# Scaled row maxima, reordered rotations and early loads in the 8-head layers of a four-part network

## The chip, the cores and the metric

The kernel runs on one core of a Trainium2 chip. The metric is the device time of one execution in microseconds. TensorE multiplies matrices, VectorE (DVE), ScalarE (ACT) and GpSimd (POOL) do the elementwise work, and SyncE (SP) issues transfers. Each engine works through its own list in order and waits on semaphores.

## The reference, cut to what matters

```python
x = x + attention0(layernorm(x))          # (8, 512, 256), one head, decay
x = x + experts(layernorm(x))             # 8 experts, one chosen for each row
x = x + attention1(layernorm(x))          # 16 heads of 16, causal
h = layernorm(x)
for l in range(2):                        # the 8-head layers: 8 heads of 64
    q, k, v = split(shift_token(h) @ wqkv[l])
    q, k = l2norm(q) * qs[l], l2norm(k) * ks[l]       # per head
    q, k = rotary_xpos(q, k)
    sim = 8 * q @ k.T                     # own window of 128 and the one before, causal
    h = h + softmax(sim) @ v @ wo[l]
    u = layernorm(shift_token(h)) * ln_g[l] + ln_b[l]
    a, g = split(u @ w1[l] + b1[l])       # 2 x 682
    h = h + (a * gelu(g)) @ w2[l] + b2[l]
x = x + h
```

## The kernel before, in words

Four phases follow one another, each a function with a block of instructions for every engine, and a barrier of all engines between them: `phase_attn0`, the routing and the experts, `phase_attn1` (the 16-head attention) and `phase_layers` (the two 8-head layers). The change touches the last two.

`phase_attn1` takes the 8 sequences in four trips of two. Its SP block (L877 to L892) loads the next trip's rows, then for each of 8 groups of heads copies rows of maxima into the queries' tile (L886), and stores its two results `x3_d` and `y_d[0]`. The second is what the layers start from. Its projection weights `w`, its rows `came` and `rows_of` (even and odd trips use different tiles) are allocated at the head of the phase.

`phase_layers` runs 16 sequences one after another (8 for each layer; `n` counts them, `HALVES` is 16). Nothing is planned by a program: the order on each engine is written out by hand in a loop over `n`. In its turn `n` an engine does the attention of sequence `n`, the feed-forward part of sequence `n - 1` and the projection of sequence `n + 1`, mixed in a fixed order. Products are made of three TensorE passes on high and low parts of both operands (`product`, L2116 to L2118).

The projection of a sequence has four tiles of 128 rows. For each tile TensorE makes queries, keys and values (`project`), ScalarE squares queries and keys (L1955) and takes the square root of the summed squares (`square_root`, L1967), VectorE turns queries and keys by rope (`turn`, L1712 and L1714), sums the squares (`norms`, L1722 and L1723) and inverts the lengths (`invert`, L1728), GpSimd adds the two halves of the turn (`add`, L1591) and scales the keys by their inverse lengths (`scale_keys`, L1529), and TensorE transposes both (`flip_qk`, L2165). The queries are not scaled: their inverse length goes into the softmax. `rotations` on each engine holds this order for tiles 1 to 3; `between` in it is the place where the normalised rows of the feed-forward part are handled (`high_rows` on ScalarE, L2045 and L2049, `low_rows` on VectorE, L1836).

The attention has 8 steps, each one window of four heads. In step `j` TensorE makes scores (L2191), VectorE adds the mask and takes four row maxima (L1771, a custom instruction that reads the scores in PSUM), then multiplies them by minus the query's inverse length (`scaled_bias`, L1766, two instructions of two columns), ScalarE takes four exponentials with that as bias and the inverse length as scale (L2001), VectorE inverts the four sums (L1779), GpSimd scales the probabilities (L1619), TensorE transposes them (L2212), ScalarE and VectorE copy them out (L2013, L1750), TensorE multiplies by the values (L2231), and after every second step ScalarE copies the result (`oT_out`, L2019). Between these TensorE has the 12 hidden products of the feed-forward part of sequence `n - 1` (L2116 to L2118). Gelu (L2033), the high and low parts of its result (L2038, L1799), the product with `wo` (L2244), the residual (L1805), the shift by one row (L2251, L2252) and the contraction with `w2` follow. GpSimd also splits `w1` and `w2` in high and low parts, once for each layer (L1640, L1643).

The phase starts with transfers of the first two sequences' rows, of `wqkv`, rope and two scale rows, then of the other weights. ScalarE waits for rope, scales and `wqkv` together (`FIRST_ALL`) before it makes the first high part (L2054).

## Time and profile before

| | |
|---|---|
| three runs | 2630.89, 2639.43, 2642.0 us; median 2639.43 |
| the profiled execution | 2633.45 us, its span 2631.7 us |
| TensorE busy | 2300.4 us, 87% of the span |
| VectorE, ScalarE, GpSimd busy | 1592.2 (60%), 1357.9 (52%), 920.2 us (35%) |
| mean granted TensorE clock | 0.932 |
| the 8-head layers | from 1208 us to the end, 54% of the span |
| one sequence in them | about 84 to 85 us |

The span is the time from the first to the last instruction in the trace; the execution is a little longer. Busy shares are averages over phases with different limits, so the rows below come from the layers themselves. An engine's line in a timeline gives, in brackets, how long it sat idle before that instruction and what ended the wait.

### The profile page before, as it was taken

How to read it: one execution, taken by the hardware profiler on the slowest of the kernel's cores; microseconds unless marked ns; L12 is line 12 of the kernel's file. 1: busy time of each engine (PE TensorE's matmuls, PEld its weight loads, DVE VectorE, ACT ScalarE, POOL GpSimd, SP SyncE). 2: the span in 40 equal slices, each digit the busy share in tenths (PEclk: the TensorE clock that was granted, in tenths of full speed). 3: DMA queues.
4: the chain of work that ended last, by engine and by line, in shares of the span. 5: the costliest groups of instructions: out<-in, count | busy, mean ns of one | idle time of the engine just before them, and what ended most of it. 6: DMA issues, size and time to landing. Idle time of an engine off the chain costs nothing.

```text
span 2631.7 us, 45273 instructions
## 1 busy us (share of the span) xinstructions
PE 2300.4 (87%) x15746; PEld 1744.6 (66%) x15746; DVE 1592.2 (60%) x5017; ACT 1357.9 (52%) x3211; POOL 920.2 (35%) x1363
## 2 busy tenths in 40 slices
PE   7999599996887878885789999999998899999997
PEld 4666599984454544534567777777767777777776
DVE  5565422225757666656567766677767766677664
ACT  1111233334656465562575567655775567566663
POOL 2221222205334343332444334433454434434441
PEclk9999799997887878787799999999999999999998
DMA  3222311102010100003000000000101000000000
GB/s 127 96 97 92 123 37 37 37 27 85 4 49 18 50 18 10 25 3 125 9 1 17 17 17 1 17 17 17 50 33 37 25 18 9 25 25 25 1 17 24
DMA packets 75937, 96.40 MB, mean 37 GB/s; under 512 B 6113, under 2 KB 69090, under 8 KB 75458
## 3 DMA queue, kind: packets, MB, share of 16 engines
q1 hardware_dynamic: 70786, 81.89, 9.2%
q0 software_dynamic: 3408, 9.31, 1.2%
q8 instruction: 130, 2.13, 0.3%
q10 hardware_dynamic: 1520, 2.31, 0.2%
q14 instruction: 93, 0.76, 0.1%
HBM read 62.69 MB, written 30.28 MB: 35 GB/s over the span
## 4 chain that ended last, share of the span: by engine, by line
PE 34%; ACT 8%; DVE 7%; issue 2%; POOL 2%; DMA 0%; SPq 0%; DVEq 0%; ACTq 0%
PE l_free L2116 5%; PE l_free L2117 5%; PE l_free L2118 5%; PE l_score L2244 4%; PE l_out L2231 3%; ACT l_probs L2001 3%; PE l_score L2191 3%; PE l_turned L2212 2%; PE l_turned L2116 2%; PE l_turned L2118 2%; PE l_turned L2117 2%; DVE l_probs L1771 2%; POOL l_probs L1619 1%; PE l_turned L2165 1%; DVE l_probsT L1714 1%
## 5 line engine op out<-in xcount | busy, mean ns | idle before, releaser
L2001 ACT ACTIVATE l_probs<-l_probs,l_nmax,l_inv 128x256 f32<-128x256 f32 (+1 forms) x512 | 287.6, 565 | 90.4 <-DVE l_nmax L1766 90.3
L1619 POOL TENSOR_SCALAR l_probs<-l_probs,l_rinv 128x256 f32<-128x256 f32 (+1 forms) x512 | 223.5, 457 | 275.3 <-DVE l_rinv L1779 275.3
L1051 DVE CUSTOM_DVE_ANT_0 c_raw<-cbank,c_later 128x256 f32<-128x256 f32 (+3 forms) x512 | 218.5, 488 | 74.2 <-PE cbank L1238 73.5
L1154 ACT ACTIVATE c_cprobsT<-cbank 128x384 f32<-128x384 f32 (+1 forms) x384 | 180.9, 524 | 92.2 <-PE cbank L1264 92.1
L1771 DVE CUSTOM_DVE_ANT_0 l_probs<-l_score,mask 128x256 f32<-128x256 f32 (+1 forms) x512 | 177.9, 385 | 22.4 <-PE l_score L2191 22.4
L2231 PE MATMUL l_out<-l_probsT,l_v 128*64 128x128 f32 x1792 | 132.1, 288 | 48.9 <-ACT l_oT L2019 48.9
L2116 PE MATMUL l_free<-l_wqkv_high,l_yT 128*128 128x512 f32 x384 | 163.9, 427 | 8.3 <-DVE l_wqkv_low L1841 8.3
L2116 PE MATMUL l_free<-l_part,l_w_high 128*128 128x512 f32 x384 | 167.2, 435 | 3.0 <-DVE l_yT L1836 3.0
L1750 DVE COPY l_probsT<-l_turned 128x512 f32<-128x512 f32 (+1 forms) x128 | 79.4, 621 | 129.3 <-PE l_turned L2212 85.3
L2117 PE MATMUL l_free<-l_wqkv_low,l_yT 128*128 128x512 f32 x384 | 157.6, 410 | 0.0
L2231 PEld LDWEIGHTS l_out<-l_probsT,l_v 128*64 128x64 f32 x1792 | 101.3, 141 | 84.3 <-ACT l_probsT L2013 69.1
L2118 PE MATMUL l_free<-l_wqkv_high,l_part 128*128 128x512 f32 x384 | 156.8, 408 | 0.0
L953 POOL TENSOR_SCALAR_AFFINE_SELECT c_cprobsT<-c_cprobsT 128x256 f32<-128x256 f32 x256 | 99.4, 411 | 161.2 <-ACT c_cprobsT L1154 158.9
L2117 PE MATMUL l_free<-l_yT,l_w_high 128*128 128x512 f32 x384 | 152.9, 398 | 0.0
L2118 PE MATMUL l_free<-l_part,l_w_low 128*128 128x512 f32 x384 | 152.6, 397 | 0.0
L718 PE MATMUL h_bank<-m_xsT,m_w1s 128*128 128x128 f32 x1248 | 147.0, 276 | 0.3 <-issue 0.3
L718 PEld LDWEIGHTS h_bank<-m_xsT,m_w1s 128*128 128x128 f32 x1248 | 143.7, 193 | 0.8 <-issue 0.7
L727 PE MATMUL y_bank<-w,m_hT 128*128 x624 | 141.0, 379 | 0.0
L2191 PE MATMUL l_score<-l_kT,l_flipped 64*128 64x256 f32 (+1 forms) x1024 | 132.1, 375 | 8.8 <-DVE l_nmax L1771 8.8
L643 POOL DMA_INDIRECT m_xs<-xn_d,source x39 | 64.4, 1651 | 212.3 <-PE xT_bank L706 179.9
L1264 PE MATMUL cbank<-c_cqT,c_ckT 64*128 64x256 f32 (+2 forms) x512 | 98.2, 416 | 46.1 <-ACT c_cprobsT L1154 39.0
L662 DVE TENSOR_TENSOR m_y<-y_bank,b 128x256 f32<-128x256 f32 x39 | 16.6, 425 | 200.4 <-PE y_bank L727 200.4
(260 smaller groups left out, 5930.9 us busy)
## 6 DMA issues: line engine op xcount, KB each, us to landing
w<-in_W1T SPq DMA_DIRECT2D x8, 1024.0 KB, 8.1
w<-in_W2T SPq DMA_DIRECT2D x8, 1024.0 KB, 11.4
l_came<-y_d SPq DMA_DIRECT2D x16, 512.0 KB, 3.8
ys_d<-m_y SPq DMA_DIRECT2D x39, 128.0 KB, 1.7
xn_d<-a_prods SPq DMA_DIRECT2D x8, 512.0 KB, 3.5
c_came<-x_d SPq DMA_DIRECT2D x8, 512.0 KB, 5.0
y_d<-c_raw SPq DMA_DIRECT2D x8, 512.0 KB, 3.7
y_d<-l_y SPq DMA_DIRECT2D x8, 512.0 KB, 2.9
```

The costliest lines, as they stand in the source:

```text
L718: last = pe.matmul(h_bank[2 * (j % 2) + h][:, f, :], w1s[j % 2][:, c, (4 * h + f) * P:(4 * h + f + 1) * P], xsT[:, j % 2, c, :], start=c = ...
L727: last = pe.matmul(y_bank[j % 2][:, 0:D], hT[:, j % 2, f, :], w, start=f == 0, stop=f == FC - 1)
L1051: last = dve.tensor_tensor_reduce(raw[:, CHUNKS - NS + s, h * 2 * P:h * 2 * P + wide], score_place("scores", u, s)[:, h * 2 * P:h * 2 * P ...
L1154: act.activation(probsT[s][:, c % 2, i, k0:k0 + w], turned_place(j, s)[:, 0:w], ACT.Exp).then_inc(probs_ready[s], 1)
L1619: pool.tensor_scalar(a, a, rinv[:, j, r, h:h + 1], 1.0, ALU.mult, ALU.mult).then_inc(normed, 1)
L1771: dve.tensor_tensor_reduce(probs[:, j % 2, r, h, 0:width], score_bank[r][:, 2 * P * h:2 * P * h + width], ban, 1.0, -3e38, ALU.add, ALU.ma ...
L2001: act.activation(a, a, ACT.Exp, bias=nmax[:, j, r, h:h + 1], scale=inv[s][:, w, head:head + 1], accum_out=rsum[:, j % 2, r, h:h + 1]).then ...
L2116: pe.matmul(out, a[0], b[0], start=start, stop=False)
L2117: pe.matmul(out, a[0], b[1], start=False, stop=False)
L2118: return pe.matmul(out, a[1], b[0], start=False, stop=stop)
L2191: last = pe.matmul(score_bank[half][:, 2 * P * h:2 * P * h + width * P], qT[s][r, p, w * P:(w + 1) * P], kT[s][r, p, k0 * P:(k0 + width) * ...
L2231: last = pe.matmul(out_bank[DH2 * half:DH2 * (half + 1), at:at + P], v[s][:, k0 + k, head:head + DH2], probsT[:, j % 2, half, 2 * h + k, : ...
```

## The change

In the layers: the maximum instruction takes the query's inverse length as its per-partition multiplier, and the query half of the inverse lengths is negated once for each sequence by a new VectorE instruction behind `rotations`, so that the maximum becomes a minimum of negated scores. The two `scaled_bias` instructions, their semaphore and the exponential's scale operand go, and ScalarE waits for each maximum alone. In `rotations` VectorE inverts, ScalarE takes the root and GpSimd scales the keys of the tile before ahead of this tile's queries, and `between` comes a tile later on ScalarE and VectorE. ScalarE copies the outputs of steps 0 and 2 before an exponential group and loads the Gelu table behind the third output copy. `wqkv` of the first layer and the first sequence's rows are loaded by SP in the last trip of `phase_attn1`, into space of tiles that are no longer used; `cx` and `came` are allocated ahead of `wo1` for that. The first two weight pieces are split ahead of the first rows. `wqkv` has a semaphore of its own, in the second layer too.

```diff
...
@@ -769,12 +769,15 @@
...
         KEYS = NT * (NT + 1) // 2 * P
+        assert nc.sbuf_base == g.early_at and PAIRS % 2 == 0
         w = sb("wqkv1", [P, DC, 3 * D])
+        even_rows = stream("cx", [P, NT, D])
+        came = stream("came", [P, NT, D])
+        assert nc.sbuf_base >= g.early_at + (DC * 3 * INNER + NT * D) * 4
+        xn = came
+        rows_of = [even_rows, stream("yrow", [P, NT, D])]
...
         rope = sb("rope1", [P, NT, 2, 2, DH1])
-        came = stream("came", [P, NT, D])
-        xn = came
-        rows_of = [stream("cx", [P, NT, D]), stream("yrow", [P, NT, D])]
@@ -877,6 +880,14 @@
...
                             sp.dma_start(came[s][:], g.x1_d[pair * NS + (NS + s)].rearrange("(t p) n -> p t n", p=P)).then_inc(x_in[s], 16)
+                    if pair == PAIRS - 1:
+                        for s in range(NS):
+                            sp.wait_ge(qk_psum[s], PAIRS * NT)
+                            sp.wait_ge(v_psum[s], PAIRS * NT)
+                            sp.wait_ge(x_stored[s], 16 * pair)
+                        sp.dma_start(g.early_wqkv[:], g.wqkv[0].rearrange("(c p) n -> p c n", p=P)).then_inc(g.early_in, 16)
+                        sp.wait_ge(y_stored[0], 16)
+                        sp.dma_start(g.early_rows[:], g.y_d[0][0].rearrange("(t p) n -> p t n", p=P)).then_inc(g.early_rows_in, 16)
@@ -1391,7 +1402,11 @@
...
 
-        wqkv_raw, wqkv = weight("wqkv", [P, DC, 3 * INNER])
+        assert nc.sbuf_base == g.early_at
+        sb("wqkv_space", [P, DC, 3 * INNER])
+        sb("rows_space", [P, NT, D])
+        wqkv_raw = g.early_wqkv
+        wqkv = [nc.alloc_sbuf_tensor_at("l_wqkv_low", [P, DC, 3 * INNER], F32R, offset=g.early_at), sb("wqkv_high", [P, DC, 3 * INNER], F32R)]
...
@@ -1480,11 +1495,10 @@
...
 
-        FIRST_ALL, TABLES, PIECES = 16 * 4, 6, DC * 3
+        FIRST_ALL, TABLES, PIECES = 16 * 3, 6, DC * 3
...
         def first_loads(layer):
-            return [(wqkv_raw[:], g.wqkv[layer].rearrange("(c p) n -> p c n", p=P)), (rope, g.rope2),
-                    (scales[:, 0, :], g.qs[layer].partition_broadcast(P)), (scales[:, 1, :], g.ks[layer].partition_broadcast(P))]
+            return [(rope, g.rope2), (scales[:, 0, :], g.qs[layer].partition_broadcast(P)), (scales[:, 1, :], g.ks[layer].partition_broadcast(P))]
@@ -1536,10 +1550,9 @@
...
 
-                for s in range(NS):
-                    sp.dma_start(came[s][:], g.y_d[0][s].rearrange("(t p) n -> p t n", p=P)).then_inc(first_in, 16)
...
                     sp.dma_start(dst, src).then_inc(w_in, 16)
+                sp.dma_start(came[1][:], g.y_d[0][1].rearrange("(t p) n -> p t n", p=P)).then_inc(first_in, 16)
@@ -1552,6 +1565,7 @@
...
                         sp.wait_ge(turned[s], pair * (6 * NT) + 6 * NT)
+                        sp.dma_start(wqkv_raw[:], g.wqkv[1].rearrange("(c p) n -> p c n", p=P)).then_inc(g.early_in, 16)
@@ -1603,11 +1617,10 @@
...
                     for t in range(1, NT + 1):
-                        if t < NT:
-                            add(n, t, 0)
...
                         if t < NT:
+                            add(n, t, 0)
@@ -1728,16 +1741,18 @@
...
                 def rotations(n, between):
+                    s, pair, _, _ = place(n)
                     for t in range(1, NT + 1):
-                        if t < NT:
-                            turn(n, t, 0)
...
                         if t < NT:
+                            turn(n, t, 0)
...
                             norms(n, t)
-                        if t == 1:
+                        if t == 2:
                             between()
+                    dve.wait_ge(inv_ready[s], pair * NT + NT)
+                    chain.step(dve.tensor_scalar(inv[s][:, :, 0:H2], inv[s][:, :, 0:H2], -1.0, None, ALU.mult))
@@ -1759,20 +1774,13 @@
...
 
-                    def scaled_bias(r):
-                        dve.wait_ge(nmax_ready, 4 * J + 2 * r + 2)
-                        cp, w = step_of(j)
-                        unit = inv[s][:, w, 4 * cp:4 * cp + 4].rearrange("p (h r) -> p r h", r=2)
-                        dve.scalar_tensor_tensor(nmax[:, j, r, :], nmax[:, j, r, :], -1.0, unit[:, r, :], ALU.mult, ALU.mult).then_inc(bias_ready, 1)
-
+                    cp, w = step_of(j)
...
                         for h in range(2):
-                            dve.tensor_tensor_reduce(probs[:, j % 2, r, h, 0:width], score_bank[r][:, 2 * P * h:2 * P * h + width], ban, 1.0, -3e38,
-                                                     ALU.add, ALU.max, nmax[:, j, r, h:h + 1]).then_inc(nmax_ready, 1)
-                            if r and h == 0:
-                                scaled_bias(0)
-                    scaled_bias(1)
+                            head = 4 * cp + 2 * h + r
+                            dve.tensor_tensor_reduce(probs[:, j % 2, r, h, 0:width], score_bank[r][:, 2 * P * h:2 * P * h + width], ban,
+                                                     inv[s][:, w, head:head + 1], 3e38, ALU.add, ALU.min, nmax[:, j, r, h:h + 1]).then_inc(nmax_ready, 1)
@@ -1842,14 +1850,14 @@
...
                     dve.memset(yT[s][:, 1, 0:1].bitcast(F32), 0.0)
-                low_parts(0)
-                dve.wait_ge(w_in, FIRST_ALL)
...
                     low_weights(0, k)
+                low_parts(0)
+                for k in range(DC, PIECES):
+                    low_weights(0, k)
+                dve.wait_ge(w_in, FIRST_ALL)
...
                     table(dve, k).then_inc(tables_ready, 1)
-                for k in range(DC, PIECES):
-                    low_weights(0, k)
@@ -1974,14 +1982,13 @@
...
                     for t in range(1, NT + 1):
-                        if t < NT:
-                            square(n, t, 0)
...
                         if t < NT:
+                            square(n, t, 0)
...
                             v_out(n, t)
-                        if t == 1:
+                        if t == 2:
@@ -1989,17 +1996,14 @@
...
                 def exps(n, j):
-                    s = place(n)[0]
                     J = n * STEPS + j
-                    cp, w = step_of(j)
-                    width = (1 + min(w, 1)) * P
+                    width = (1 + min(step_of(j)[1], 1)) * P
                     for r in range(2):
-                        act.wait_ge(bias_ready, 2 * J + r + 1)
                         for h in range(2):
-                            head = 4 * cp + 2 * h + r
+                            act.wait_ge(nmax_ready, 4 * J + 2 * r + h + 1)
                             a = probs[:, j % 2, r, h, 0:width]
-                            act.activation(a, a, ACT.Exp, bias=nmax[:, j, r, h:h + 1], scale=inv[s][:, w, head:head + 1],
-                                           accum_out=rsum[:, j % 2, r, h:h + 1]).then_inc(probs_ready, 1)
+                            act.activation(a, a, ACT.Exp, bias=nmax[:, j, r, h:h + 1], scale=-1.0, accum_out=rsum[:, j % 2, r, h:h + 1])\
+                               .then_inc(probs_ready, 1)
@@ -2050,11 +2054,13 @@
...
                     if k == 0:
-                        act.wait_ge(w_in, (layer + 1) * FIRST_ALL)
+                        act.wait_ge(g.early_in, 16 * (layer + 1))
...
 
+                for k in range(DC):
+                    high_weights(0, k)
                 rows_out(0)
-                for k in range(PIECES):
+                for k in range(DC, PIECES):
@@ -2062,14 +2068,12 @@
...
                         if att:
+                            if p in (5, 7):
+                                oT_out(n, (p - 5) // 2)
...
                                 exps(n, p - 1)
-                            if ffn and p == 8:
-                                act.preload_act_table(ACT.Gelu)
...
                                 pT_out(n, p - FLIP_LAG)
-                            if p in (5, 7):
-                                oT_out(n, (p - 5) // 2)
@@ -2081,6 +2085,8 @@
...
                         oT_out(n, 2)
+                    if att and ffn:
+                        act.preload_act_table(ACT.Gelu)
@@ -2122,7 +2128,7 @@
...
                     else:
-                        pe.wait_ge(first_in, 16 * NS)
+                        pe.wait_ge((g.early_rows_in, first_in)[s], 16)
@@ -2454,6 +2460,10 @@
...
             phase_experts(nc, g)
+        g.early_at = -(-nc.sbuf_base // 32) * 32
+        g.early_wqkv = nc.alloc_sbuf_tensor_at("early_wqkv", [P, DC, 3 * INNER], F32, offset=g.early_at)
+        g.early_rows = nc.alloc_sbuf_tensor_at("early_rows", [P, NT, D], F32, offset=g.early_at + DC * 3 * INNER * 4)
+        g.early_in, g.early_rows_in = g.once("early_in"), g.once("early_rows_in")
```

## Rows read from the trace of the kernel before

**Rows 1.** windows, one sequence's period each: busy us, PEclk, DMA share, GB/s
```profile
1436.00:1521.00 85.00, 79.16 (x590) 63.26 (x590) 58.70 (x186) 53.71 (x128) 32.04 (x49) 0.98 0.04 14
1521.00:1605.00 84.00, 77.78 (x590) 62.05 (x589) 59.23 (x185) 53.37 (x128) 31.99 (x49) 1.00 0.04 14
```

**Rows 2.** waits from 1300 us on: waiter, releaser; total us, times, longest
```profile
PE l_turned L2165 <- POOL l_work L1529: 30.0, 15, 2.5
PE l_out L2231 <- ACT l_oT L2019: 44.7, 45, 3.5
PE l_turned L2212 <- POOL l_probs L1619: 14.8, 30, 0.8
PE l_score L2191 <- DVE l_nmax L1771: 4.5, 9, 0.6
```

**Rows 3.** timeline, PE, two sequences: start, duration, instruction, idle before it
```profile
1498.11 0.63 PE L2117 MATMUL l_free<-l_wqkv_low,l_yT 128*128 128x512 f32 x1
1591.45 1.13 PE L2191 MATMUL l_score<-l_kT,l_flipped 64*128 64x256 f32 x8 [0.48 <-DVE l_nmax L1771]
```

**Rows 4.** timeline, DVE, scaling of two maxima in one step
```profile
1433.01 0.45 DVE L1766 SCALAR_TENSOR_TENSOR l_nmax<-l_nmax,l_inv 128x2 f32<-128x2 f32 x1
```

**Rows 5.** timeline, ACT, same stretch
```profile
1433.49 0.60 ACT L2001 ACTIVATE l_probs<-l_probs,l_nmax,l_inv 128x256 f32<-128x256 f32 x1 [1.54 <-DVE l_nmax L1766]
1456.12 1.28 ACT L2068 ACT_TABLE_LOAD   x1
1461.94 0.62 ACT L2038 ACTIVATE l_u_high<-l_work 128x512 fp32r<-128x512 f32 x1
```

**Rows 6.** timeline, POOL, same stretch
```profile
1436.25 1.85 POOL L1619 TENSOR_SCALAR l_probs<-l_probs,l_rinv 128x256 f32<-128x256 f32 x4 [2.10 <-DVE l_rinv L1779]
```

**Rows 7.** line L1766: durations in ns, min/median/max
```profile
L1766 DVE SCALAR_TENSOR_TENSOR l_nmax<-l_nmax,l_inv x256: 154/171/3500, 1250.2 to 2559.8; 128x2 f32<-128x2 f32 x128
```

**Rows 8.** groups by form, DVE, from 1213 us on: count, busy us, mean ns
```profile
L79 DVE TENSOR_SCALAR l_v<-l_out,l_mv,l_rstd 128x128 f32<-128x128 f32 x64 | 25.9, 405 | 0.0
L1771 DVE CUSTOM_DVE_ANT_0 l_probs<-l_score,mask 128x128 f32<-128x128 f32 x128 | 31.4, 282 | 0.0
```

**Rows 9.** timeline, ACT, POOL and DVE between two projections
```profile
1488.76 1.45 ACT L2045 ACTIVATE l_hT<-l_score,l_lng 128x512 f32<-128x512 f32 x2
...
1495.50 1.04 POOL L1529 TENSOR_TENSOR l_work<-l_work,l_inv 128x512 f32<-128x512 f32 x1
...
1588.23 1.12 DVE L1723 TENSOR_SCALAR l_ss<-l_ss 128x16 f32<-128x16 f32 x1
1589.63 0.25 DVE L1728 RECIPROCAL l_inv<-l_root 128x16 f32<-128x16 f32 x1 [0.28 <-ACT l_root L1967]
...
1590.03 1.04 POOL L1529 TENSOR_TENSOR l_work<-l_work,l_inv 128x512 f32<-128x512 f32 x1 [0.71 <-DVE l_inv L1728]
```

**Rows 10.** chain of waits in the first sequence: start, us, what
```profile
1264.11 2.40 DVE l_nmax L1766
1282.08 3.04 DVE l_nmax L1766
```

**Rows 11.** timeline where the 8-head layers begin
```profile
1208.26 0.92 SPq L1540 DMA_DIRECT2D l_came<-y_d  x2
1221.46 3.23 ACT L2054 ACTIVATE l_wqkv_high<-l_wqkv_raw 128x512 fp32r<-128x512 f32 x6 [5.49 <-DMA l_scales<-in_ks]
1227.29 0.68 DVE L1712 TENSOR_TENSOR l_probs<-l_free,l_scaled 128x512 f32<-128x512 f32 x1
```

**Rows 12.** DMA issues at that start: count, KB, us to landing
```profile
l_came<-y_d SPq DMA_DIRECT2D x2, 512.0 KB, 4.2
l_scales<-in_ks SPq DMA_DIRECT2D x1, 32.0 KB, 10.7
```

**Rows 13.** timeline, PE and SP, last trip of the 16-head attention
```profile
1080.30 1.95 PE L1193 MATMUL cbank<-c_wqkv,c_cprobsT 128*128 128x512 f32 x4
...
1104.83 11.23 SPq L886 DMA_DIRECT2D c_cqT<-c_nmaxT  x8
```

More of the change, by code:

```diff
@@ L29 @@
 EPS = 1e-5
-LOOP_SEMS = 150
+LOOP_SEMS = 154
 class Chain:
```

4 lines of the change are left out of this document (2 added, 2 removed).

## The prediction

> **What bounds the kernel now.** I read the busy shares in 40 slices first, then windows cut at the 8-head layers' repetitions, the waits of that stretch, and last the timelines of single engines. The reader should see a pipeline with little room: 16 sequences pass one after another, each covers the attention of one sequence and the feed-forward part of the one before it, and TensorE is busy for 79.2 of 85 us [rows 1]. No other engine is near that, so TensorE's gaps set the time. From 1300 us on they have three owners [rows 2]: the second key tile's transposes wait for GpSimd's scaled keys (30.0 us in 15 waits, 2.0 a sequence), the probability-times-value products for ScalarE's copy of the output bank (44.7 in 45, 3.0 a sequence), the transposes of probabilities for GpSimd's scaling (14.8 in 30, 1.0 a sequence). A fourth is small, the second score product for the row maxima (4.5 in all).
>
> **The clock.** Behind the 2.0 us gap the 512-column products ran at 0.63 instead of 0.40 us [rows 3], the lower level of 1.2 GHz. Of 14 windows 8 show a granted clock of 0.98 and 6 show 1.00 [rows 1]. They were cut at the same place of each sequence and are 85 and 84 us long; I take 0.7 us for a fall, and that the falls go with the gap: 8 x 0.7 = 6 us.
>
> **Part 1, the length in the maximum.** Each of 8 steps a sequence loses two small VectorE products (256 in all, 285 ns mean, 154 at least, 3500 at most [rows 7]); the four maxima take the length as a per-partition multiplier instead of the constant 1.0. ScalarE, which idled 1.54 us for that product before the exponential of 1433.49 [rows 5], now starts behind the first maximum, not behind two and their product (1433.01 plus 0.45 [rows 4]). The first maximum ends two maxima, 0.7 us, before 1433.01, so at about 1432.3: exponentials start near 1432.45, 1.0 us sooner. GpSimd's scaling at 1436.25 had idled 2.10 us for the reciprocals behind them [rows 6] and follows: it ends at 1437.1, and TensorE's gap there, 1.0 a sequence, goes. The exponential takes -1.0 for its scale where it took a length: I count nothing; ScalarE is hidden behind TensorE's hidden-layer products, and without that cover it is under 0.05 us each.
>
> The new multiplier is not in the trace. The nearest pair is 282 ns for a maximum of 128 columns and 405 ns for a subtract-and-scale of as many with two per-partition operands [rows 8]: from 0 to 0.12 us more each, or at worst a second pass. I take 0.03; the exponentials come every 0.59 us and hide it, except in the first step (4 x 0.03, counted below).
>
> **Part 2, the output copies.** The copies for steps 0 and 2 move ahead of an exponential group, and the Gelu table load (1.28 us at 1456.12 [rows 5]) moves behind the third copy. What queues behind the moved copies on ScalarE are the exponentials of steps 4 and 6: the copy waits for TensorE's product, by my reckoning until 1439.5 and 1447.7, the exponentials go on at 1440.1 and 1448.3, and their scaled probabilities are ready at 1444.2 and 1452.85 where TensorE asks at 1445.3 and 1453.0. The cover is 1.1 us for the one and 0.15 us for the other, the thinnest in this sum; with it gone the loss is what the copy comes later, one to one. Of the 3.0 us a sequence [rows 2] the first two gaps go, of the third (the table load in it) about 0.7 us stays, since the copy then follows its product directly. Parts 1 and 2 together would bring the last product forward by 3.25 us. But the feed-forward stage behind it is ScalarE's and VectorE's: table load, two Gelus, row copies, then the high part at 1461.94 [rows 5]. I put that at 1459.45, 2.5 sooner, and the residual rows that the shifting product needs had 0.35 us to spare. So 2.8 us count: 15 sequences x 2.8 = 42 us.
>
> **Part 3, the rotations.** Now ScalarE does the two affine and two high copies of the normalised rows (1.45 us for the first pair at 1488.76, 2.5 in all) before the keys' square roots and squares, and GpSimd adds the next tile's queries before it scales the keys at 1495.50 [rows 9]. In the new order length, inverse and key scaling of tile 1 come first: the keys are ready near 1492.3, TensorE asks at 1494.5, the 2.0 us gap goes. Late next: the normalised rows' copies sit between tile 2 and tile 3, so ScalarE squares tile 3's queries 1.7 us behind TensorE, and the first hidden product waits 0.5 us for their turn. Then the last lengths, with a tensor-scalar of 1.12 us that waits for GpSimd's add [rows 9], inverse, the new negation (0.2 us; nearest, the inverse's 0.25), and four first maxima. In the sequence without a clock fall the second score product began at 1591.45, when the first maxima had ended [rows 3]; I put it at 1589.8 to 1589.95. That VectorE chain, not the 2.0 us gap, is the gain: 1.5 us x 15 = 23 us, from 0.5 to 2.0 each.
>
> The added multiplication by -1 uses the inverses in SBUF while GpSimd is about to scale keys (1.04 us [rows 9]). That small tensor-scalar operations do wait for a GpSimd instruction the row of 1.12 us for 16 columns shows. The Trainium skill, SBUF — State Buffer, section "Who interferes with whom", says that such an operation in a two-port mode and a GpSimd instruction lock each other out and that the first to start wins; the trace agrees. VectorE is ready about 0.03 us behind the inverse, GpSimd started 0.15 us behind it (1589.63 plus 0.25, to 1590.03 [rows 9]), so I let VectorE win.
>
> **Part 4, the first sequence and the weight splits.** Twice in the first sequence the small product waited for GpSimd's splitting of the weights, 2.40 and 3.04 us on the chain [rows 10]; the maxima read PSUM and a mask and did not wait there. Without feed-forward work to cover it the steps are a bare chain, so I add 1 us for earlier exponentials and 1.2 for the keys: 2.4 + 3.0 + 1 + 1.2, say 7.5. The 3500 ns [rows 7] is the same in sequence 9, half covered: 1.5. From 2 to 11 for both.
>
> **Part 5, the loads.** At the start of the layers rows are asked for at 1208.26, the weights' high parts start at 1221.46 when the last small table lands, and the first turn is at 1227.29 [rows 11]. Weights and first rows are now there at 1208.3. The turn still needs rope and scales: issued within the first 1.5 us with less ahead of them than before, they land between 4.2 us (512 KB of rows) and 10.7 us (the scale row) after [rows 12]; I take 5.5, so 1215, then 1.6 us for the tables: first turn at 1216.6, gain 10.5, from 5 to 12. Weights (six copies of 0.54, six subtractions of 0.62) finish by 1214.2, under that. In the last trip of the 16-head attention the transfers are issued behind the last projection (1082.3); the next small row transfer on SP is at 1104.83 [rows 13], 22 us on, and 2 MB took under 10 us in every place of this trace. So nothing is queued behind them in time: 0, at most 1 us.
>
> **The sum.** 42 + 23 + 6 + 7.5 + 1.5 + 10.5 = 90.5 us off the profiled execution's own 2633.45 us gives 2543. The median of the three runs is 2639.43, 6 us above it. With fewer clock falls the spread should shrink, so I add half: 2546 us.
>
> **Rivals.**
> A. GpSimd wins the port at the negation: it ends 1.0 us later, and the second score product with it: 15 us back, 2561. For it: a margin of 0.1 us. This is also what the skill's rule gives if "first to start" goes the other way.
> B. The multiplier is read over the path that the small products wait for: four maxima a step instead of two products, each losing 285 - 154 = 0.13 us: 0.52 a step, some 6 steps on the chain, 3.1 a sequence, 47 us back: 2593. Against: per-partition operands beside a PSUM source stand in rows of ordinary length [rows 8]. Part 2's cover of 0.15 us giving out works in the same direction.
> C. Slower than before: the multiplier costs the maximum a second pass, 0.35 us each at 256 columns. Eight steps carry 1.4 us more on VectorE, near TensorE's own 4.1 us a step; the attention stage loses 1.05 us in seven steps where it gained 2.8, and the first maxima lose 0.8. Per sequence 7.3 + 0.8 - 1.5 = 6.6 lost, 99 in 15, less 18 for start and clock: 2639 + 81 = 2720. It decides from about 0.2 us a maximum on. Against: the rows of 8.
> D. The attention stage gains nothing at the end because the high parts and the residual hold as now; only parts 3 to 5 count: 2588. TensorE's wait for the shifted rows would then grow by what part 1 and 2 give.
>
> **Chances.** Forecast 0.55 (own range 2530 to 2556), A 0.14, B 0.11, D 0.13, C 0.04, no effect within bound 0.03. Bounds of the unknowns (rotations 0.5 to 2.0, start 5 to 12, splits 2 to 11) reach from 2535 to 2574 around the forecast; with A, B and D the range is 2520 to 2600. About 0.5% (13 us) is what a measurement of this kernel can tell from no change: faster by more 0.93, within 0.03, slower by more 0.04.
>
> **What would show it.** Part 1: exponentials start behind the first maximum, and TensorE's wait for scaled probabilities vanishes. Part 2: waits for the output copy fall from 3.0 to about 0.7 a sequence. Part 3: no wait for scaled keys, granted clock 1.00 in nearly all windows, and in its place waits of 0.5 and 0.8 us at the first hidden and the second score product. Part 5: first turn near 8 us behind the layers' start. It is wrong if a 256-column maximum takes over 0.6 us, if the negation takes 1 us or more, if a sequence's period stays above 82 us, or if the exponentials of steps 4 and 6 are waited for by TensorE.

## The result, and the profile after

The changed kernel takes 2543.68 us (median of 4 runs, 2543.18 to 2549.92); the kernel before took 2635.16 us in the same series. The ratio is 0.966, 95% interval 0.9624 to 0.9695. The forecast was 2546.

The profiled execution took 2549.92 us, its span is 2548.2. It is the slowest of the four, and it reached the 8-head layers at 1217.6 us, the kernel before at 1208.3. That is no cost of the change: the same stores on SP were 4.6 us late at 204 us already, and the first product of the 16-head attention came 11.0 us late (619.6 against 608.6), all of it in phases that the change does not touch. Over the fourteen kernels of this study the layers began anywhere from 1205.5 to 1217.7. I therefore compare the layers' phase, from VectorE's first memset in it to the end of the span: 1423.4 us before, 1330.5 after, 92.9 gained.

The page after, busy time and slices (columns as in the page before):

```profile
PE 2288.1 (90%) x15746; PEld 1738.7 (68%) x15746; DVE 1544.3 (61%) x4777; ACT 1312.5 (52%) x3211; POOL 921.1 (36%) x1363
...
PE   7999599996788887878699999999999999999997
...
PEclk9999699998788988878899999999999999999998
```

Windows of two sequences, cut from one transposing of normalised rows to the next (against [rows 1]):

```profile
1466.04:1545.56 79.52, 77.29 (x590) 61.94 (x588) 56.65 (x170) 50.62 (x127) 32.13 (x50) 1.00 0.05 14
1545.56:1625.20 79.64, 77.48 (x589) 61.98 (x588) 56.53 (x170) 50.65 (x127) 32.01 (x50) 1.00 0.04 15
```

TensorE does the same instructions in 77.4 us (77.8 in the window before that has the same clock), with a granted clock of 1.00 in both windows; its gaps are 2.2 us a sequence where they were 6.2 in that window (84.00 less 77.78). TensorE's waits from 1300 us on (against [rows 2]):

```profile
PE l_out L2237 <- ACT l_oT L2023: 11.8, 15, 0.8
PE l_score L2197 <- DVE l_nmax L1782: 10.7, 15, 0.7
PE l_turned L2122 <- DVE l_u_low L1807: 9.0, 1, 9.0
PE l_free L2122 <- DVE l_probsT L1727: 6.5, 15, 0.5
...
PE l_turned L2218 <- POOL l_probs L1632: 4.1, 16, 1.2
```

The wait for scaled keys is gone from the list; the copy of the output bank is waited for once a sequence (0.79 us) instead of three times (3.0), scaled probabilities for 0.3 us instead of 1.0. In their place stand the 0.71 and 0.43 us for maxima and last turn that the prediction put at 0.8 and 0.5. The 9.0 us are the splitting of the feed-forward weights in one sequence, as before.

Groups by form, ScalarE's exponentials and VectorE's maxima (count, busy us, mean ns, idle before), against [rows 8], and in a second fence the durations of the smallest operations (ns, min/median/max), the tensor-scalar on sums of squares and the negation:

```profile
L2005 ACT ACTIVATE l_probs<-l_probs,l_nmax 128x256 f32<-128x256 f32 x384 | 190.4, 499 | 26.0 <-DVE l_nmax L1782 26.0
...
L1782 DVE CUSTOM_DVE_ANT_0 l_probs<-l_score,mask,l_inv 128x256 f32<-128x256 f32 x384 | 163.2, 481 | 27.8 <-PE l_score L2197 27.7
L1782 DVE CUSTOM_DVE_ANT_0 l_probs<-l_score,mask,l_inv 128x128 f32<-128x128 f32 x128 | 36.8, 345 | 0.6
```

```profile
L1736 DVE TENSOR_SCALAR l_ss<-l_ss x64: 174/238/256, 1229.0 to 2442.7; 128x16 f32<-128x16 f32 x64
...
L1755 DVE TENSOR_SCALAR l_inv<-l_inv x16: 181/181/185, 1244.2 to 2443.6; 128x32 f32<-128x32 f32 x16
```

No tensor-scalar on the sums waits for GpSimd any more (1.12 us in [rows 9]). The same two groups by form of the kernel before:

```profile
L2001 ACT ACTIVATE l_probs<-l_probs,l_nmax,l_inv 128x256 f32<-128x256 f32 x384 | 226.0, 591 | 82.7 <-DVE l_nmax L1766 82.6
...
L1771 DVE CUSTOM_DVE_ANT_0 l_probs<-l_score,mask 128x256 f32<-128x256 f32 x384 | 146.5, 419 | 22.4 <-PE l_score L2191 22.4
```

And the place where the last lengths, negation and key scaling meet (timeline, DVE, POOL, PE; the counterpart of [rows 3, 9]):

```profile
1560.74 0.25 DVE L1741 RECIPROCAL l_inv<-l_root 128x16 f32<-128x16 f32 x1 [0.28 <-ACT l_root L1975]
1561.02 0.18 DVE L1755 TENSOR_SCALAR l_inv<-l_inv 128x32 f32<-128x32 f32 x1
1561.24 0.35 DVE L1782 CUSTOM_DVE_ANT_0 l_probs<-l_score,mask,l_inv 128x128 f32<-128x128 f32 x1
...
1561.13 1.04 POOL L1543 TENSOR_TENSOR l_work<-l_work,l_inv 128x512 f32<-128x512 f32 x1 [0.71 <-DVE l_inv L1741]
...
1562.57 1.13 PE L2197 MATMUL l_score<-l_kT,l_flipped 64*128 64x256 f32 x8 [0.71 <-DVE l_nmax L1782]
```

VectorE started 0.11 us ahead of GpSimd, and in all 16 sequences the negation took 0.18 us. GpSimd was not held either: its scaling took 1.04 us beside the negation in each of the 16, as in the kernel with the late negation, where the two don't overlap. At the start of the layers (timeline, SP and DVE):

```profile
1217.59 0.35 SPq L1554 DMA_DIRECT2D l_work<-in_rope  x1
...
1223.58 0.49 DVE L1529 TENSOR_TENSOR l_scaled<-l_work,l_scales 128x128 f32<-128x128 f32 x2 [0.24 <-DMA l_scales<-in_ks]
...
1225.18 0.69 DVE L1725 TENSOR_TENSOR l_probs<-l_free,l_scaled 128x512 f32<-128x512 f32 x1
```

The first turn comes 7.6 us behind the layers' first request on SP, where it was 19.0 in [rows 11].

**Where the 92.9 us came from**, by the starts of TensorE's transposes of normalised rows (one group for each sequence; a period is the time from one to the next), with VectorE's first memset as the start:

| stretch | before | after | gained | predicted |
|---|---|---|---|---|
| start to first turn | 19.0 | 7.5 | 11.4 | 10.5 |
| first turn to transposes, 1st sequence | 88.9 | 79.8 | 9.1 | 7.5 + 2.8 |
| 15 periods | 1269.4 | 1196.7 | 72.7 | 39.2 + 23 + 6 + 1.5 |
| what is left behind them | 46.1 | 46.5 | -0.4 | 0 |

The 42 us of parts 1 and 2 stand here as 2.8 and 39.2. An undisturbed period fell from 83.9 to 79.6 us: 4.3, which is the 2.8 and 1.5 of the prediction. 15 x 4.3 is 64.5; the 8.2 us left are clock falls, the weight splits and the last period (7.5 predicted for the first two).

### The profile page after: what moved, and what is told of

The parts are those of the page before. It is cut to its first block, busy times and chain, and to the rows that moved or that the text cites. A ratio compares the mean times of both kernels' runs of the same rounds, so it can differ in the third digit from the quotient of the medians.

```text
span 2548.2 us, 45050 instructions
## 1 busy us (share of the span) xinstructions
PE 2288.1 (90%) x15746; PEld 1738.7 (68%) x15746; DVE 1544.3 (61%) x4777; ACT 1312.5 (52%) x3211; POOL 921.1 (36%) x1363
## 4 chain that ended last, share of the span: by engine, by line
PE 27%; DVE 9%; ACT 8%; issue 5%; POOL 3%; DMA 0%; DVEq 0%; SPq 0%; POOLq 0%; ACTq 0%
PE l_free L2122 4%; PE l_free L2124 3%; PE l_free L2123 3%; PE l_out L2237 3%; PE l_score L2197 2%; POOL l_probs L1632 2%; PE l_turned L2218 2%; DVE l_work L1801 2%; DVE l_probsT L1727 2%; DVE l_u_low L1807 2%; PE l_turned L2122 1%; PE l_turned L2124 1%; PE l_turned L2123 1%; ACT l_probs L2005 1%; PE l_turned L2171 1%
## 5 line engine op out<-in xcount | busy, mean ns | idle before, releaser
L2005 ACT ACTIVATE l_probs<-l_probs,l_nmax 128x256 f32<-128x256 f32 (+1 forms) x512 | 240.0, 474 | 26.0 <-DVE l_nmax L1782 26.0
L1782 DVE CUSTOM_DVE_ANT_0 l_probs<-l_score,mask,l_inv 128x256 f32<-128x256 f32 (+1 forms) x512 | 200.0, 447 | 28.4 <-PE l_score L2197 27.7
L1765 DVE COPY l_probsT<-l_turned 128x512 f32<-128x512 f32 (+1 forms) x128 | 79.8, 624 | 132.6 <-PE l_turned L2218 81.8
L2123 PE MATMUL l_free<-l_wqkv_low,l_yT 128*128 128x512 f32 x384 | 152.1, 396 | 0.0
L1275 PE MATMUL cbank<-c_cqT,c_ckT 64*128 64x256 f32 (+2 forms) x512 | 97.3, 413 | 46.5 <-ACT c_cprobsT L1165 39.2
L693 ACT ACTIVATE m_hT<-h_bank,m_b1s 128x128 f32<-128x128 f32 x312 | 88.9, 368 | 85.1 <-PE h_bank L718 73.2
## 6 DMA issues: line engine op xcount, KB each, us to landing
w<-in_W2T SPq DMA_DIRECT2D x8, 1024.0 KB, 11.4
```

The lines of the kernel that those rows point to most:

```text
L1782: dve.tensor_tensor_reduce(probs[:, j % 2, r, h, 0:width], score_bank[r][:, 2 * P * h:2 * P * h + width], ban, inv[s][:, w, head:head + 1] ...
L2005: act.activation(a, a, ACT.Exp, bias=nmax[:, j, r, h:h + 1], scale=-1.0, accum_out=rsum[:, j % 2, r, h:h + 1])\
L2123: pe.matmul(out, a[0], b[1], start=False, stop=False)
```

## The experiments

Each ratio compares a kernel with the kernel before in the same series. There were four series, with before at 2634.4 to 2638.6 us, and the changed kernel was measured in the first alone; so a difference to it in medians can be off by some 3 us (without part 3 it is 33 us by the medians and 30 by the ratios). "Period" is the commonest undisturbed distance between two such transposes, "phase" the layers' phase, each from one trace; both are free of the scatter of earlier phases.

| kernel | us | ratio (95%) | phase | period |
|---|---|---|---|---|
| before | 2634 to 2639 | 1 | 1423.4 | 83.9 |
| the change | 2543.7 | 0.966 (0.9624-0.9695) | 1330.5 | 79.6 |
| part 5 alone | 2620.4 | 0.9949 (0.993-0.9967) | 1412.7 | 83.9 |
| part 3 alone | 2599.3 | 0.9868 (0.985-0.9886) | 1386.2 | 82.35 |
| part 1 alone | 2586.4 | 0.982 (0.9802-0.9838) | 1372.4 | 81.85 |
| part 2 alone | 2612.3 | 0.9922 (0.9902-0.9941) | 1399.6 | 82.5 |
| without part 3 | 2577.1 | 0.9774 (0.9753-0.9795) | 1365.5 | 81.15 |
| without part 2 | 2545.5 | 0.9652 (0.9632-0.9672) | 1334.9 | 80.35 |
| without part 1 | 2566.7 | 0.9737 (0.9715-0.976) | 1354.9 | 80.95 |
| scale from a column | 2541.5 | 0.963 (0.961-0.965) | 1327.8 | 79.4 |
| late negation | 2570.0 | 0.9755 (0.9739-0.9771) | 1358.8 | 80.9 |
| rows' transposes first | 2537.4 | 0.9629 (0.9612-0.9646) | 1327.4 | 79.6 |
| first maxima first | 2527.0 | 0.9589 (0.9574-0.9604) | 1314.4 | 78.85 |
| all three | 2526.5 | 0.9586 (0.9567-0.9606) | 1313.9 | 78.85 |

### The parts alone

**Part 5** (before, with the diff's hunks of the loads):

```
+                        sp.dma_start(g.early_wqkv[:], ...).then_inc(g.early_in, 16)
+                        sp.dma_start(g.early_rows[:], ...).then_inc(g.early_rows_in, 16)
```

> The kernel before with part 5 alone: the weights and the first rows of the 8-head layers are loaded in the last trip of the 16-head attention, the tables behind them, the order of the first splits changed. Theory (the prediction's own term): the first turn comes 10 us sooner behind the start of the layers, and nothing else moves: 10 us off, about 2628 beside 2638 for before. Rival 1: the first turn was not what held the layers' start (projections of the weights' later pieces are), and 3 to 5 us come off. Rival 2: the transfers of 2 MB in the last trip delay the 16-head attention's own row transfers by some us, and the sum is 0 to 5 us.

14 us came off by the medians, 10.7 by the phase, which is the theory. The first turn came 7.6 us behind the start. The 16-head attention was not longer: from its first product to the layers it took 594.3 us, where before took 599.7 and the kernels with that phase unchanged took 594 to 600. So the transfers of its last trip cost nothing that these traces can tell. Rivals 1 and 2 fall.

**Part 3** (before, with the new order, no negation; GpSimd's hunk, VectorE and ScalarE are changed alike):

```
-                        if t < NT:
-                            add(n, t, 0)
                         if t >= 2:
                             scale_keys(n, t - 1)
                         if t < NT:
+                            add(n, t, 0)
                             add(n, t, 1)
```

> The kernel before with part 3 alone: the new order of the rotations on VectorE, ScalarE and GpSimd; maxima, exponentials and output copies as before, no negation. Theory: TensorE's gap of 2.0 us for the scaled keys goes, the granted clock stays at 1.00, and the way from the normalised rows' transposes to the first scores shortens by the 2.1 us a sequence that it shortened by in the whole change: 15 x 2.1 = 31 us off, about 2607. Rival 1: the attention stage behind it, which waits for GpSimd's scaling and ScalarE's copies, hands the gain back because these waits grow (GpSimd and ScalarE are then not earlier by as much): 10 to 15 us off. Rival 2: without the later steps nothing is gained but the clock, 6 us.

35 us came off by the medians, 37.1 by the phase. That is a little over the theory, for a period gains 1.55 us against an undisturbed one and the falls of the clock behind the rotations go with it. All of the 1.55 lies between the normalised rows' transposes and the second scores; from there to the last product of probabilities and values it is 43.1 us as before, so the attention stage handed nothing back. No period shows the clock's fall behind the rotations (two fall elsewhere).

**Part 1** (before, with the new maxima, exponentials and negation):

```
+ chain.step(dve.tensor_scalar(inv[s][:, :, 0:H2], ..., -1.0, None, ALU.mult))
+ inv[s][:, w, head:head + 1], 3e38, ALU.add, ALU.min, nmax[...]).then_inc(nmax_ready, 1)
- dve.scalar_tensor_tensor(nmax[:, j, r, :], ..., unit[:, r, :], ALU.mult, ALU.mult)
+ act.activation(a, a, ACT.Exp, bias=nmax[...], scale=-1.0, ...)
```

> The kernel before with part 1 alone: the length as the maximum's multiplier, the constant -1 as the exponential's scale, the small products gone, one negation of the lengths a sequence. Theory: the wait for scaled probabilities (1.0 us a sequence) goes and the first gap for the output copy shrinks with the earlier exponentials (about 1.0 of 3.0), the two stalls of the first sequence go (5.4 to 7.5) and that of sequence 9 (1.5): 15 x 2 + 8 = 38 us off, about 2600. Rival 1: parts 1 and 2 only work together, because ScalarE's copies still stand behind the exponentials that follow them: 15 x 1 + 8 = 23 off, about 2615. Rival 2: part 1 carries nearly all of the 2.9 us a sequence that the attention stage gained: 15 x 2.9 + 8 = 51 off, about 2587. In this order the negation meets GpSimd's scaling of the last keys as in the whole change; 1 us or more for it would say that the order of the rotations decides who wins the port.

48 us came off, nearly what rival 2 said. A period gains 2.05 us, and the first sequence ends 9.2 us sooner. Its waits from 1300 us on and three periods, the first and two later ones:

```profile
PE l_turned L2158 <- POOL l_work L1529: 30.0, 15, 2.5
PE l_out L2224 <- ACT l_oT L2012: 25.8, 45, 1.4
```

```profile
1308.33:1393.51 85.18, 79.43 (x589) 63.20 (x589) 61.29 (x179) 50.86 (x127) 32.34 (x50) 0.98 0.04 14
...
1475.32:1557.22 81.90, 77.33 (x590) 61.90 (x589) 58.23 (x170) 50.85 (x127) 31.97 (x50) 1.00 0.04 14
1557.22:1639.06 81.84, 77.60 (x590) 61.95 (x588) 58.04 (x170) 50.87 (x127) 31.89 (x50) 1.00 0.04 14
```

Earlier exponentials alone take the waits for the output copy from 3.0 to 1.7 us a sequence. And the gap of 2.0 us for scaled keys is there in all 15 sequences, but the clock fell behind it only in the first period (0.98 above). In none of the 14 later ones did it fall there, where it did in 7 of before's. The expectation also asked whether the order of the rotations decides who goes first at the negation. It does not: in this order, too, VectorE started 0.11 us ahead of GpSimd and the negation took 0.18 us, in all 16 sequences.

**Part 2** (before, with the output copies and the table load moved):

```
+                            if p in (5, 7):
+                                oT_out(n, (p - 5) // 2)
                             if 0 < p <= STEPS:
                                 exps(n, p - 1)
-                            if ffn and p == 8:
-                                act.preload_act_table(ACT.Gelu)
...
+                    if att and ffn:
+                        act.preload_act_table(ACT.Gelu)
```

> The kernel before with part 2 alone: output copies of steps 0 and 2 ahead of an exponential group, the Gelu table load behind the third copy; small products as before. Theory: the first two gaps for the output copy (2.0 us a sequence) go, but the exponentials behind the moved copies start later by up to 0.6 us where scaled probabilities are already 1.0 us a sequence late, so about half is kept: 15 x 1.2 = 18 us off, about 2620. Rival 1: the parts are independent and it gives 15 x 2.3 = 35 off, about 2603. Rival 2: the exponentials fall behind by all that the copy waits, and nothing or less than nothing comes off: 2632 to 2645.

22 us came off, 1.4 us a period, between the theory and rival 1.

### One part undone

**Without part 3** (the changed kernel, with the order of before on three engines):

```
+                        if t < NT:
+                            add(n, t, 0)
                         if t >= 2:
                             scale_keys(n, t - 1)
                         if t < NT:
-                            add(n, t, 0)
                             add(n, t, 1)
```

> The changed kernel with part 3 undone: rotations in the order of before, the one negation a sequence kept. Alone the four parts gave 14, 35, 48 and 22 us, 119 together, and the whole gives 91.5: 28 us are earned twice. Theory: the double counting lies between parts 1 and 2, which shorten the same stretch from scores to the last product, and part 3 is independent of both: undone it costs its 35 us, about 2578. Rival 1: it lies between part 3 and part 1 (the clock, and first maxima that come sooner either way): undone it costs 20 to 25 us, about 2566.

33 us slower than the changed kernel by the medians, 35.0 by the phase. The undisturbed period is 81.15, so the order of the rotations is worth 1.55 us alone and on top alike: the theory, part 3 is independent of the others. The rest of the 35 us is the clock: in 8 of the 14 later periods it fell behind the gap of 2.0 us, and the stretch from the normalised rows' transposes to the first scores takes 14.9 instead of 13.4 us. One such period and one without:

```profile
1628.71:1711.30 82.59, 79.08 (x589) 63.16 (x588) 57.97 (x170) 50.76 (x127) 32.09 (x50) 0.98 0.04 14
1711.30:1792.43 81.13, 77.64 (x589) 61.96 (x588) 57.82 (x170) 50.78 (x127) 31.91 (x50) 1.00 0.04 14
```

**Without part 2:**

```
-                    if att and ffn:
-                        act.preload_act_table(ACT.Gelu)
...
-                            if p in (5, 7):
-                                oT_out(n, (p - 5) // 2)
                             if 0 < p <= STEPS:
                                 exps(n, p - 1)
```

> The changed kernel with part 2 undone: output copies behind the exponentials of the same step and the Gelu table load before the third copy, as before. Alone part 2 gave 22 us. Theory: with the small products gone the copies were nearly in time, so part 2 is worth less here, 5 to 10 us: about 2551. Rival 1: it is worth its 22 us here too: 2565. Rival 2: more, since a feed-forward stage that starts sooner was waiting for it: 2570 and above.

Neither theory nor rivals: the ratio, 0.9652, can't be told from 0.966, and the phase is 4.4 us longer. The period is 0.75 longer (80.35). Its wait, from 1300 us on:

```profile
PE l_out L2237 <- ACT l_oT L2023: 25.8, 45, 1.4
```

TensorE waits 1.72 us a sequence for output copies instead of 0.79, but from the end of the last product of probabilities and values to the next transposes it takes 22.0 to 22.1 us instead of 22.4. That gives a third back; that it is so because the Gelu table load stands ahead of the copy again, and the feed-forward stage starts sooner, is my reading and not tested by itself. 11 us should come of 14 periods; the first sequence ended 3.65 us sooner than in the changed kernel's trace. Since kernels with the same first sequence scatter there by 2 to 3 us, I don't put that down to part 2.

**Without part 1:**

```
+ dve.scalar_tensor_tensor(nmax[:, j, r, :], ..., unit[:, r, :], ALU.mult, ALU.mult)
- act.activation(a, a, ACT.Exp, bias=nmax[...], scale=-1.0, ...)
+ act.activation(a, a, ACT.Exp, bias=nmax[...], scale=inv[s][:, w, head:head + 1], ...)
```

> The changed kernel with part 1 undone: maxima with 1.0, the small products back, exponentials scaled by the length, no negation. Alone part 1 gave 48 us. Theory: parts 1 and 2 share most of what they give, so it costs 30 to 35 us here: about 2577. Rival 1: it is independent and costs 48: 2591. Rival 2: the first steps of a sequence, where part 3 brings the scores sooner, hide the products, and it costs 20 or less: 2563 or below.

23 us by the medians, 24.5 by the phase: between the theory and rival 2. The period is 1.35 us longer. Parts 1 and 2 together give 2.75 us (the period without part 3 against before), 2.05 and 1.4 alone: 0.7 us is the overlap, both ways. Together the four parts' kernels gain 122.6 us by the phase where the change gains 92.9. Of the 29.7 earned twice, this overlap is 10 to 11 in 15 periods. Some 10 more lie in the disturbances of the periods, mostly falls of the clock: the kernels with part 3 alone and part 1 alone both lack before's falls in the 14 later periods. Some 8 lie ahead of the first sequence's transposes, where parts 5, 1 and 3 gained 14.5, 9.2 and 4.2 us alone and the change 20.5.

### The disputed costs

**The exponential's scale.**

```
- bias=nmax[:, j, r, h:h + 1], scale=-1.0,
+ bias=nmax[:, j, r, h:h + 1], scale=minus_one[:, 0:1],
```

> The changed kernel with the exponential's scale of -1 read from a column in SBUF instead of the constant. In the changed kernel's trace the exponential of 128x256 takes 499 ns and the one of 128x128 397 ns where before they took 591 and 489; 0.09 us less each, 0.37 a step, which the prediction counted as nothing. Theory: the 0.09 us is the reading of a per-partition scale, and it hid behind TensorE: the exponentials are back at 591 and 489 ns and the time rises by under 8 us. Rival 1: the exponentials are on the path, four of them before GpSimd's scaling in the first step and the last one: 0.37 x 2 x 15 = 11 us and more. Rival 2: the 0.09 us has another cause (what is read on VectorE or in what order), and the durations stay at 499 and 397 with the column too.

```profile
L2007 ACT ACTIVATE l_probs<-l_probs,l_nmax,l_minus_one 128x256 f32<-128x256 f32 x384 | 225.8, 591 | 15.8 <-DVE l_nmax L1783 15.8
L2007 ACT ACTIVATE l_probs<-l_probs,l_nmax,l_minus_one 128x128 f32<-128x128 f32 x128 | 61.5, 489 | 0.0
```

This shows the cause: 591 and 489 ns are back to the nanosecond, so the 92 ns are the reading of a per-partition scale, and all 47 us of it on ScalarE are hidden, as the theory had it. Only the first sequence, which has no cover, ends 3.1 us later, 1.6 of which are tables that landed late. That the period is 0.2 us shorter I can't explain.

**Rival A, forced.**

```
                     dve.wait_ge(inv_ready[s], pair * NT + NT)
+                    dve.wait_ge(k_rotated[s], pair * NT + NT)
                     chain.step(dve.tensor_scalar(inv[...], -1.0, None, ALU.mult))
```

> The changed kernel with the negation of the lengths made to wait until GpSimd has scaled the last keys: the order that rival A of the prediction described, forced. In the changed kernel the negation (0.18 us) started 0.11 us ahead of GpSimd's 1.04 us, in all sequences. Theory: the first maxima, and with them TensorE's second score product, come 1.1 us later in every sequence: 15 x 1.1 = 17 us over the changed kernel, about 2560, and TensorE's wait for the maxima grows from 0.7 to 1.8 us. Rival: the exponentials, not the maxima, hold the steps behind, and only part of it counts: 5 to 8 us over.

26 us over the changed kernel, more than the theory. Its wait for the maxima from 1300 us on, the negation in one sequence, and two sequences' windows:

```profile
PE l_score L2198 <- DVE l_nmax L1783: 30.0, 15, 2.2
```

```profile
1558.35 0.18 DVE L1756 TENSOR_SCALAR l_inv<-l_inv 128x32 f32<-128x32 f32 x1 [1.29 <-POOL l_work L1543]
```

```profile
1378.20:1460.64 82.44, 79.04 (x589) 63.04 (x588) 56.62 (x170) 50.63 (x127) 31.99 (x50) 0.98 0.04 14
1460.64:1541.63 80.99, 77.31 (x589) 61.95 (x588) 56.84 (x170) 50.62 (x127) 32.13 (x50) 1.00 0.04 14
```

The wait grew from 0.7 to 2.0 us, 1.3 a sequence, 19 us in all. In nine of the fifteen periods the clock fell behind it, which made a period 1.55 us longer: 14 us. (The phase is 28.2 us longer and not 33; the last period and the end behind it lack 3.9 us that the changed kernel's trace has there.) A product in the first of these windows, timeline of PE:

```profile
1399.04 0.63 PE L2124 MATMUL l_free<-l_yT,l_w_high 128*128 128x512 f32 x1
```

So the order of rival A costs about 26 us, not 15: 1.3 us a sequence and not 1.0, and the clock. Here a semaphore held the negation. Whether GpSimd, had it started first, would have held it in the changed kernel is not shown: in the 16 cases where the two overlapped, by 0.07 us, neither took longer than alone.

### Two more edits, and all together

**Rows' transposes first** (TensorE):

```
-                    if att:
-                        output(n, STEPS - 2)
                     if more:
                         flip_rows(n + 1)
                     if att:
+                        output(n, STEPS - 2)
```

> The changed kernel with the transposes of the next sequence's rows ahead of the last but one output product on TensorE. That product waits 0.79 us a sequence for ScalarE's copy of the output bank, and the transposes (1.0 us) fit there. Theory: the wait goes; of the 0.79 us a sequence about 0.5 counts, since the Gelus and high parts on ScalarE stay where they are and the products behind then wait for them: 14 x 0.5 = 7 us off the changed kernel, about 2536. Rival 1: all of it counts, 11 us. Rival 2: none does, since the feed-forward stage behind sets the end.

```profile
PE l_out L2257 <- DVE l_y L1813: 12.0, 13, 1.0
```

Rival 2 was right: the wait for the output copy (0.79) is gone, the shifting product waits 0.9 us for the residual rows instead, and the period stays at 79.6. The 6 us between the medians sit in the first sequence and in scatter (phase: 3.1).

**First maxima first** (VectorE, within the last tile's turn and norms):

```
+ chain.step(dve.tensor_scalar(inv[s][:, 0:t, 0:H2], ..., -1.0, None, ALU.mult))
  turn(n, t, 0)
  turn(n, t, 1)
+ row_max(n, 0)
  norms(n, t)
...
- if p < STEPS:
+ if 0 < p < STEPS:
      row_max(n, p)
```

> The changed kernel with the first step's maxima on VectorE ahead of the last tile's norms: they need only the first tile's lengths. The lengths of tiles 0 to 2 are negated in one instruction before the last tile's turn, those of tile 3 behind their inverse. Theory: the maxima end 2 us sooner, TensorE's 0.7 us wait before the second score product goes; the last lengths, the table load behind their root and the first exponentials come 1.1 us later, which is covered by the hidden products (8 us until the probabilities' first transposes are asked for): 15 x 0.7 = 10.5 us off, about 2533. Rival 1: the exponentials and the copies behind them on ScalarE are late instead, and the wait moves to the first transposes or the third hidden product: 0 to 4 us off. Rival 2: the negation ahead of the turn meets GpSimd's scaling of tile 2 and costs 1 us a sequence: 5 us slower.

```profile
PE l_out L2242 <- ACT l_oT L2028: 11.8, 15, 0.8
PE l_turned L2127 <- DVE l_u_low L1812: 9.0, 1, 9.0
PE l_free L2127 <- DVE l_probsT L1727: 7.1, 15, 0.5
```

The wait for maxima left the list and nothing took its place: 0.72 us a period, as the theory said, 10 us in 14 periods. 2526.97 us is 17 under the changed kernel (phase: 16.1); the other 6 us lie in the first and the last sequence and behind it. There kernels that hardly differ scatter too (the changed kernel and the one with the scale from a column by 3.9 us in the last period and behind it), so I count 10 as shown.

**All three:** both edits, and

```
-                            if p in (5, 7):
+                            if ffn and p in (5, 7):
                                 oT_out(n, (p - 5) // 2)
...
+                            if not ffn and p in (5, 7):
+                                oT_out(n, (p - 5) // 2)
```

> Both changes of the two kernels before, and in the first sequence, which has no feed-forward work beside it, the output copies behind the exponentials as in the kernel before the change (undoing part 2 brought the first sequence's end 3.65 us sooner). Theory: the three are independent: 7 + 10.5 + 3.6 = 21 us off the changed kernel, about 2523. Rival: the earlier attention stage meets ScalarE's Gelus and high parts, so only one of the two waits is won: 12 us off, 2532.

In the first sequence this puts the output copies behind the exponentials again. The kernel takes 2526.5 us. By its mechanism the rival was right: the gains don't add, and the period stays at 78.85. Its time of 2532 was not, since the second edit brought 17 us by the medians where 10.5 had been expected. The second edit alone carries the gain; the first moves a wait, and the copies' order in the first sequence shows no gain in the whole.

## Why the prediction was right

Forecast 2546, measured 2543.68. What held and what didn't, by its steps:

- **The bound** (TensorE's gaps set the time) held: of the 4.3 us that a period lost, about 4 were gaps and 0.4 busy time (77.8 to 77.4).
- **Parts 1 and 2, 2.8 us a sequence**: 2.75 measured in the kernel without part 3. That only 2.8 of 3.25 would count, since the feed-forward stage's start holds, is borne out by the kernel without part 2 (0.93 us more waiting, 0.75 longer period) and by the moved transposes, where the whole 0.79 us went into the wait for the residual. So the limit that rival D described begins just behind this change. The cover of 0.15 us for step 6 held in 14 of 15 sequences. In the ninth period TensorE waited 1.24 us for scaled probabilities, and 0.44 in the kernel without part 2: it gave out once, for 0.8 us.
- **The multiplier**: 0.062 us (419 to 481, 282 to 345 ns) where I took 0.03, inside 0 to 0.12, hidden as said: the second scores come 17.0 us behind the transposes, as with part 3 alone, which has the old maxima. B and C fall with the row: the maxima were not held by GpSimd (319 to 486 ns in all 512).
- **The exponential**: counted as nothing, "under 0.05 us"; it is 0.092 us shorter. Mis-sized, without effect.
- **Part 3, 1.5 us**: 1.55. The waits that replace the gap were named with their sizes (0.5 and 0.8; 0.43 and 0.71).
- **Rival A**: the margin was as thin as said (0.11 us) and VectorE started first 16 of 16 times. The price was too low: the wait grew by 1.3 us, not 1.0, and I left out the clock.
- **The clock, 6 us**: the size about held, though not by its terms: before's falls behind the gap made six of the later periods 0.66 to 1.54 us longer, 6.0 in all, where the sum had eight at 0.7. The reason given ("the falls go with the gap") holds by half. Without the gap there was no fall behind the rotations in any kernel. With it they may still not come: part 1 alone keeps the gap and shows one fall behind it, in the first period, and none in the 14 later ones; the kernel without part 3 has the same gap and falls in 8 of the 14 (part 5 alone in 9, part 2 alone in 5, before in 7); the late negation brings falls by another gap of 2.0 us. What else decides was not settled.
- **Part 4**: 9.1 us for the first sequence behind the first turn, 10.3 predicted (7.5 and the 2.8 of parts 1 and 2). **Part 5**: 11.4 by the first turn, 10.7 by its own kernel, 10.5 predicted.

The Trainium skill, SBUF — State Buffer, section "Who interferes with whom", was cited for the first to start winning the lock. The trace does not contradict it and does not show it for this pair: the negation started first and took 0.18 us, but GpSimd's 1.04 us beside it are its 1.04 us without it. The other side (GpSimd first) was avoided by a wait in the forced kernel, so no run here shows it with the negation. What the traces do show is the row of 1.12 us in [rows 9]: the same instruction takes at most 0.26 us in the changed order.

## What to carry to other kernels

Sum gaps of the bounding engine, but count at each what stands next behind: the gap for scaled keys was 2.0 us and its removal gave 1.55, with waits of 0.4 and 0.7 us in its place. Parts that shorten the same stretch share their gain (0.7 of 3.45 us), so that one of them may be worth little beside the other. When a small operation is on the chain only because of its place in an engine's order, ask which data it needs: the first maxima needed only the first tile's lengths, and moving them took another 0.72 us off every period.

## What was unexpected of the hardware

- An exponential with a constant scale took 499 ns (128x256) and 397 ns (128x128), with a per-partition scale from SBUF 591 and 489: 92 ns at both widths, gone and back with the operand alone.
- A maximum with a constant multiplier took 282 and 419 ns (128 and 256 columns), a minimum with a per-partition one 345 and 481: 62 to 63 ns more at both widths, so no second pass. The multiplier and the change to a minimum were not measured apart.
- Behind a gap of 2.0 us a sequence on TensorE the lower clock (0.63 us a product) came in 5 to 9 of the 14 later periods of five kernels and in none of a sixth, part 1 alone. Where it came, the period was 0.7 to 1.8 us longer than an undisturbed one with the same gap.
- The negation on VectorE (0.18 us) and GpSimd's scaling of the keys (1.04 us), which began 0.11 us later and reads the same tile in SBUF, each took as long as without the other, 16 times of 16.
